# A selective scan on one core: three of sixteen products u·B per chunk move to GpSimd, its products with C are written in place in a ring of eight states, and C is broadcast and copied two states later

## The reference, cut to what matters

```python
dt = softplus(dt_low @ dt_proj_w.T + dt_proj_b)
dA = exp(dt[..., None] * A)
dBx = dt[..., None] * Bc[:, :, None, :] * xc[..., None]
def step(h, inp):
    dA_t, dBx_t, C_t = inp
    h = dA_t * h + dBx_t
    return (h, einsum('bds,bs->bd', h, C_t))
y = ys + D * xc
y = y * silu(z)
```

## Time and profile before

| | |
|---|---|
| median of 3 executions | 6006.07 us (6005.42 to 6010.8) |
| the profiled execution, its own time | 5990.85 us |
| its span | 5989.1 us |
| DVE busy in the span | 5104.7 us (85%) |
| PE busy | 4802.9 us (80%) |
| ACT busy | 3730.3 us (62%) |
| POOL busy | 1754.4 us (29%) |
| the scan of the first image | from 228 to 702 us |

### The profile page before, as it was taken

One profiled execution on the slowest core, in us unless ns is written; L12 is line 12 of the kernel. 1 busy time (PEld: TensorE's weight loads), 2 busy tenths in 40 slices (PEclk: granted clock), 3 DMA queues, 4 the chain that ended last, 5 costly groups with the idle time before them and its releaser, 6 DMA issues. The chain is left out here.

```text
span 5989.1 us, 76415 instructions
## 1 busy us (share of the span) xinstructions
PE 4802.9 (80%) x21528; PEld 1760.4 (29%) x21592; DVE 5104.7 (85%) x6562; ACT 3730.3 (62%) x4769; POOL 1754.4 (29%) x1306
## 2 busy tenths in 40 slices
PE   5767779998666777999867677799986767789997
PEld 2222422223322242222332224222233222422223
DVE  6799779998779977999868996799987899679998
ACT  1666368883266636888326663788832666378882
POOL 3488500000148850000014885000001588400000
PEclk8899989999889998999988999899988899989998
DMA  1000020000000002000000000200000000020000
GB/s 38 0 1 0 15 54 0 0 0 22 22 0 1 0 15 54 0 0 0 22 22 0 1 0 15 54 0 0 0 22 22 0 1 0 15 54 0 0 0 15
DMA packets 26646, 69.25 MB, mean 12 GB/s; under 512 B 11224, under 2 KB 13088, under 8 KB 23328
## 3 DMA queue, kind: packets, MB, share of 16 engines
q1 hardware_dynamic: 26400, 66.43, 4.4%
HBM read 26.55 MB, written 8.39 MB: 6 GB/s over the span
## 5 line engine op out<-in xcount | busy, mean ns | idle before, releaser
L1257 ACT ACTIVATE arena<-ps 128x1024 f32<-128x1024 f32 x2048 | 1982.8, 1024 | 282.7 <-PE ps L1228 242.0
L1272 DVE TENSOR_TENSOR arena<-arena 128x1024 f32<-128x1024 f32 x1664 | 1913.9, 1220 | 130.3 <-ACT arena L1257 130.2
L916 DVE TENSOR_TENSOR_SCAN arena<-ps,hlast,arena 128x512 f32<-128x512 f32 x1024 | 1267.3, 1281 | 5.2 <-DVE arena L898 3.2
L876 POOL TENSOR_TENSOR arena<-arena 128x1024 f32<-128x1024 f32 x512 | 1206.9, 2357 | 22.6
L1228 PE MATMUL ps<-arena 128*128 (+1 forms) x4096 | 1079.8, 384 | 87.5 <-issue 61.6
L1212 PE MATMUL ps<-arena 128*32 128x512 f32 x8192 | 1077.0, 603 | 38.2 <-DVE arena L1277 35.2
L845 ACT ACTIVATE ps<-arena,amat 128x512 f32<-128x512 f32 x1024 | 692.0, 688 | 508.2 <-DVE arena L916 507.5
L813 PE MATMUL ps<-arena,ident 128*128 128x512 f32 x2048 | 970.2, 597 | 7.7 <-POOL arena L876 7.7
L1572 POOL MEMSET arena<- 128x1024 f32 x4 | 3.8, 956 | 2771.8 <-POOLq L101 2771.8
L1228 PEld LDWEIGHTS ps<-arena 128*128 128x128 f16 x4096 | 316.1, 98 | 1194.6 <-ACT arena L1257 807.1
L898 DVE TENSOR_TENSOR arena<-arena,ps 128x1024 f32<-128x1024 f32 x512 | 618.4, 1208 | 45.2 <-remote 30.9
(11 more groups left out here) (242 smaller groups left out, 4402.5 us busy)
## 6 DMA issues: line engine op xcount, KB each, us to landing
arena<-x SPq DMA_DIRECT2D x32, 512.0 KB, 5.9
arena<-arena SPq DMA_DIRECT2D x64, 256.0 KB, 6.0
arena<-arena SPq DMA_DIRECT2D x64, 224.0 KB, 5.8
arena<-pe SPq DMA_DIRECT2D x256, 32.0 KB, 1.8
out<-arena SPq DMA_DIRECT2D x8, 1024.0 KB, 3.9
expw<-L_ffn_expert_w SPq DMA_DIRECT2D x1, 512.0 KB
wqkv<-L_attn_W_qkv SPq DMA_DIRECT2D x1, 192.0 KB
wx<-in_projT SPq DMA_DIRECT2D x1, 128.0 KB
```

The lines of the kernel that those rows point to most:

```text
L876: pool.tensor_tensor(halves(g[s % 4]), halves(hb[s % 4]), cs[s % 4].unsqueeze(1).broadcast_to([128, HD, CH]), ALU.mult).then_inc(hc_s, 1)
L916: dve.tensor_tensor_scan(halves(hb[s % 4])[:, h, :], da(s, h), halves(dbx[s % 2])[:, h, :], k.hlast[:, s, h, :], ALU.mult, ALU.add).then_i ...
L1257: act.activation(probs[p % 8], k.bank(2 * group[p], 2 * CH), ACT.Exp, scale=SCALE / SPLIT ** 2).then_inc(exp_s, 1)
L1272: dve.tensor_tensor(acc[p % 2], acc[p % 2], probs[p % 8], ALU.add).then_inc(acc_s, 1)
```

## The change

POOL now also computes the products u·B of states 8, 12 and 15 ("lent" states). For each, PE broadcasts B_s into the bank of C, ACT copies it to SBUF (`bs`), and POOL multiplies it with u into one of two new tiles (`dbp`), from which DVE scans. `LOANED` gives for each of these states the step in which B is spread and copied, and the step after whose product with C POOL does the multiplication. The states stand in a ring of eight tiles, and POOL writes h·C over the state itself. ACT, not POOL, saves the last column. C_s is broadcast and copied at step s+2, and `total` comes six states later instead of four. The pieces of the next chunk's preparation stand at other states: rounding behind state 4 (was 8), the three softplus parts behind 6, 8 and 10 (were 10, 11, 12), 1+x at 3 (was 7), Ln at 6 (was 10).

```diff
-    dbx, hb, g = low[0:2], low[2:6], low[6:10]
+    dbx, hb = low[0:2], low[2:10]
+    RING, LATE, CLATE = len(hb), 6, 2
...
+    LOANED = {8: (2, 2), 12: (5, 7), 15: (8, 9)}
+    SOFTPLUS = (6, 8, 10)
...
 # tensor
+                    if s - 1 in spread_at:
+                        pe.wait_ge(lent_s, lent(c, spread_at[s - 1]) + 1)
...
+                    if s >= CLATE:
+                        spread_c(c, s - CLATE, q)
...
+                    if s >= LATE:
+                        total(c, s - LATE)
...
+                    if s in spread_at:
+                        pe.matmul(k.bank(C_BANK), k.sel[:, spread_at[s], :], pieces[q], start=True, stop=True).then_inc(lent_mm, 1)
             chunks(body, pe)
-            for s in range(DS - 4, DS):
+            for s in range(DS - CLATE, DS):
+                spread_c(NCH - 1, s, 1)
+            for s in range(DS - LATE, DS):
                 total(NCH - 1, s)
...
 # scalar
+                    act.activation(k.hlast[:, (s - 2) % DS, :, :], halves(hb[(s - 2) % RING])[:, :, CH - 1:CH], ACT.Copy).then_inc(hl_s, 1)
+                    if s >= CLATE:
+                        copy_c(c, s - CLATE)
...
+                    if s in spread_at:
+                        p = spread_at[s]
+                        act.wait_ge(lent_mm, lent(c, p) + 1)
+                        act.wait_ge(lent_dbx, lent(c, p) + (2, 0, 1)[loans.index(p)])
+                        act.activation(bs[loans.index(p) % 2], k.bank(C_BANK), ACT.Copy).then_inc(lent_s, 1)
...
 # gpsimd
-                    pool.tensor_copy(k.hlast[:, s, :, :], halves(hb[s % 4])[:, :, CH - 1:CH]).then_inc(hl_s, 1)
...
-                    pool.tensor_tensor(halves(g[s % 4]), halves(hb[s % 4]), cs[s % 4].unsqueeze(1).broadcast_to([128, HD, CH]),
+                    pool.tensor_tensor(halves(hb[s % RING]), halves(hb[s % RING]), cs[s % 4].unsqueeze(1).broadcast_to([128, HD, CH]),
                                        ALU.mult).then_inc(hc_s, 1)
+                    if s in inject_at:
+                        p = inject_at[s]
+                        wait(lent_s, lent(c, p) + 1)
+                        pool.tensor_tensor(halves(dbp[loans.index(p) % 2]), halves(u[q]), bs[loans.index(p) % 2].unsqueeze(1).broadcast_to([128, HD, CH]),
+                                           ALU.mult).then_inc(lent_dbx, 1)
...
 # vector
-                        if h == 0 and s < DS - 1:
+                        if h == 0 and s < DS - 1 and s + 1 not in LOANED:
                             inject(c, q, s + 1)
-                    if more and s == 8:
+                    if more and s == 4:
                         steps.vector_rounding(dve, c + 1)
-                    if s == 2 and not first(c):
+                    if s == LATE - 2 and not first(c):
                         finish(c - 1)
```

More of the change, by code:

```diff
@@ L549, in __init__ @@
         self.ab, self.onep, self.rx = take(HD * CH), take(HD * CH), take(HD * CH)
-        self.rest = self.onep[:, 0:CH]
+        self.rest = take(CH)
         self.pieces = [take(CH // 2).bitcast(BF16) for _ in range(2)]
@@ L776, in scan, with owned, lent @@
     low = [k.at(a, HD * CH) for a in range(DBC_AT + L, STEPS_AT, HD * CH)]
-    dbx, hb, g = low[0:2], low[2:6], low[6:10]
+    dbx, hb = low[0:2], low[2:10]
+    RING, LATE, CLATE = len(hb), 6, 2
     cs = [low[10 + i // 2][:, (i % 2) * CH:(i % 2 + 1) * CH] for i in range(4)]
-    assert steps.end <= ARENA
+    bs = [low[12][:, i * CH:(i + 1) * CH] for i in range(2)]
+    dbp = [k.at(steps.end + i * HD * CH, HD * CH) for i in range(2)]
+    assert steps.end + 2 * HD * CH <= ARENA
+    LOANED = {8: (2, 2), 12: (5, 7), 15: (8, 9)}
+    SOFTPLUS = (6, 8, 10)
+    loans = sorted(LOANED)
+    spread_at = {LOANED[p][0]: p for p in loans}
+    inject_at = {LOANED[p][1]: p for p in loans}
+    NL, OWN = len(loans), DS - len(loans)
+    def owned(s):
+        return s - sum(p < s for p in loans)
+    def lent(c, p):
+        return c * NL + loans.index(p)
     dt, u, pieces, dt_s, rx_s, pc_s = steps.dt, steps.u, steps.pieces, steps.dt_s, steps.rx_s, steps.pc_s
@@ L783, in scan @@
         "b_mm", "c_mm", "y_mm", "da_ready", "dbx_ready", "scan_done", "hlast_saved", "hc_ready", "c_copied", "chunk_done"))
+    lent_mm, lent_s, lent_dbx = (k.sem(n) for n in ("lent_b_mm", "lent_b_copied", "lent_dbx_ready"))
     def da(s, h):
@@ L806, in total @@
             def total(c, s):
-                pe.wait_ge(hc_s, c * DS + (s + 5))
+                pe.wait_ge(hc_s, c * DS + (s + 1))
                 if s == 0:
@@ L812, in total, with spread_c @@
                 for h in range(HD):
-                    last = pe.matmul(k.bank(Y_BANK + h), k.ident[:, :], halves(g[s % 4])[:, h, :], start=False, stop=s == DS - 1)
+                    last = pe.matmul(k.bank(Y_BANK + h), k.ident[:, :], halves(hb[s % RING])[:, h, :], start=False, stop=s == DS - 1)
                 last.then_inc(y_mm, 1)
+            def spread_c(c, s, q):
+                if s >= 1 or not first(c):
+                    pe.wait_ge(cs_s, c * DS + s)
+                pe.matmul(k.bank(C_BANK), k.sel[:, DS + s, :], pieces[q], start=True, stop=True).then_inc(c_mm, 1)
             def body(c, q, more):
@@ L838, in _, with copy_c @@
         def _(act):
+            def copy_c(c, s):
+                n = c * DS + s
+                act.wait_ge(c_mm, n + 1)
+                if s >= 4 or not first(c):
+                    act.wait_ge(hc_s, n - 3)
+                act.activation(cs[s % 4], k.bank(C_BANK), ACT.Copy).then_inc(cs_s, 1)
             def body(c, q, more):
@@ L845, in body @@
                         act.activation(da(s, h), halves(dt[q])[:, h, :], ACT.Exp, scale=k.amat[:, h, s:s + 1]).then_inc(da_s, 1)
[L846 to L852, removed]
+                    act.activation(k.hlast[:, (s - 2) % DS, :, :], halves(hb[(s - 2) % RING])[:, :, CH - 1:CH], ACT.Copy).then_inc(hl_s, 1)
+                    if s >= CLATE:
+                        copy_c(c, s - CLATE)
+                    elif not first(c):
+                        copy_c(c - 1, s - CLATE + DS)
+                    if s in spread_at:
[3 more added lines that the diff above has]
+                        act.activation(bs[loans.index(p) % 2], k.bank(C_BANK), ACT.Copy).then_inc(lent_s, 1)
                     if more and s < HD:
@@ L855, in body @@
                     if more and s == 2:
+                        steps.scalar_high(act, c + 1, 1 - q)
                         steps.scalar_exp(act, c + 1)
                     if more and s == 3:
+                        steps.scalar_one_plus(act, c + 1)
+                    if more and s == 5:
                         steps.scalar_middle(act, c + 1, 1 - q)
-                    if more and s == 7:
-                        steps.scalar_one_plus(act, c + 1)
-                    if more and s == 10:
+                    if more and s == 6:
                         steps.scalar_log(act, c + 1)
+            act.wait_ge(k.sem("h_zero"), 3)
             chunks(body, act)
+            for s in range(DS - CLATE, DS):
+                copy_c(NCH - 1, s)
         @block.gpsimd
@@ L881, in body @@
                         steps.pool_low(pool, c + 1, 1 - q)
[L882 to L888, removed]
+                    if more and s in SOFTPLUS:
+                        steps.pool_softplus(pool, c + 1, 1 - q, SOFTPLUS.index(s))
+            for last in hb[RING - 2:RING]:
+                pool.memset(halves(last)[:, :, CH - 1:CH], 0.0).then_inc(k.sem("h_zero"), 1)
+            pool.memset(k.hlast[:, 0:DS - 2, :, :], 0.0).then_inc(k.sem("h_zero"), 1)
+            pool.wait_ge(k.sem("h_zero"), 3)
+            pool.sem_inc(hl_s, DS - 2)
             chunks(body, pool)
```

45 lines of the change are left out of this document (25 added, 20 removed).

## The result

| | before | after |
|---|---|---|
| median | 6008.43 us (6005.42 to 6010.87) | 6113.15 us (6109.96 to 6118.54) |
| span of the profiled execution | 5989.1 us | 6108.1 us |

The ratio is 1.0175, with a 95% interval of 1.0158 to 1.0193. The change makes the kernel slower by about 105 us. The forecast was 64 us faster, and its range ended at 5977.

A forecast was written before the change was run, and what follows sets the result against it. DVE was taken to set the pace in the scan. Injects -107, rounding +39, image ends +14 and image starts -10 sum to -64 us, so 6006 became 5942, rounded to 5943, with a range of 5900 to 5977.

The forecast's parts named there:

- What bounds the kernel, and the injects: Scan: DVE sets the pace; three injects less save 3.33 us a chunk, 107 us in all, period 54.9.
- POOL's rate: Scan: POOL operations follow every 2.30 us, in place too; 52.8 us a chunk fits under 54.9, load 96%.
- the lower bound of 0.1: Column copy on ACT: taken as 0.2 us, bounded by 0.1 and 0.3.
- The moved rounding: Behind state 4, DVE's rounding sits out one POOL operation: 1.4 us a chunk, 39 us given back over 28 roundings.
- the bound of 2.2: Most the rounding would lose a chunk, in us, if a POOL operation starts just ahead of it.
- The end of an image: Six sums queued behind the last C broadcast: finish starts 8.5 us after the scans, 14 us lost in all.
- The start: First chunk of each image: DVE's 14.3 us wait goes as C comes later; gain 10 us, bounds 0 and 14.
- No collision: Rival, 15%: a POOL boundary falls by the rounding, so all 39 us stay: 5904.
- "slower" rival: Rival, 5%: ten POOL operations from product 6 to next chunk's u hold back the inject of state 0: 6020.

The follow-up runs named there:

- the first two experiments: Changed kernel with one rounding input in PSUM, its correction left out: 5912.06 us; changed kernel with POOL waiting for the rounding before lent product 8: 5918.62 us.
- the experiment with the old places: Changed kernel with the rounding, Ln and three softplus parts back at the states where they stood before: 6151.94 us, ratio 1.0254.
- the last one: Changed kernel with POOL waiting before lent product 8, finish ahead of the rounding, and two sums earlier at an image's end: 5903.83 us, ratio 0.9845.

## Why the prediction was wrong, point by point

- **What bounds the kernel, and the injects: right.** DVE sets the pace in the scan, and with the stretch taken away the chunk runs as forecast: where POOL waits ahead of the lent product of state 8, the roundings of two chunks without a wait for B start at 412.76 and 467.55 (54.8 apart; 54.9 was forecast).
- **POOL's rate: right.** Its operations keep the spacing of 2.30, in place too, and its mean load fits: busy for 53.18 of those 54.79 us, 97% where 96% was given. The column copy on ACT, for which 0.2 was taken, has a mean of 191 ns, but the copy of C starts 0.1 behind its start (300.51 and 300.60 in the changed kernel), so it adds the lower bound of 0.1. The first product of the chunk starts 11.0 into it, where 10.9 was given.
- **The moved rounding: the step that failed.** "The rounding must sit out the rest of it and ends near 20.0 instead of 18.6: 1.4 a chunk." The place and the partner of the collision were right (ready at 17.43 in the chunk against 17.4, in the lent product of state 8), and also the cause, shown by the kernel with one operand in PSUM. The length was not. The text itself names POOL's operations there "all back to back", and yet prices one of them. The price came from the project stage, where an idle time of 0.27 and 0.18 stands before POOL's operations, as each waits for the one ahead. In the scan there is no gap between POOL's operations, as the earlier trace rows shows (338.80 comes 2.31 behind 336.49, which lasts 2.35). In all 28 chunks of the changed kernel DVE got in only when POOL ran dry, and the bound of 2.2 that I gave as the highest was none. Measured: a stretch of 6.5 a chunk, 181 us in all where 39 stood in the sum. The kernel with a gap between two POOL operations brings the stretch to 1.8 a chunk (89.7 us for its 32 executions), near the forecast's 1.4.
- **Who waits for the delayed instruction: not followed.** `finish` is queued behind the rounding, the first sum waits for it on PE, and the sum runs at the lower clock, so that B comes late. That was 46.5 us of waits, absent from the prediction's sum. The kernel with `finish` first shows where they come from: with the rounding between `finish` and the inject, 7 are left. Why the clock is low there is not shown. Not all of it is owed to the stretch: with a rounding of 1.2 us in the same place 20.0 were left.
- **The end of an image: right.** 34.0 us of idle time ahead of the four last `finish`, 8.5 each, as forecast. **The start: right** as far as the old wait goes: the 14.3 us of the earlier trace rows are gone from the first chunk, all of them, where the sum took 10.
- **The rivals.** "No collision" is what the first two experiments made, at 5912 and 5919, by the ratio 5923 and 5930 (5904 was given, without the waits for B). The "slower" rival named another mechanism, POOL's chain to u. It did not act in the changed kernel, but does in the experiment with the old places (78.7 us) and, by 1.4 us, in the last one. The rival that should have stood there is the collision itself, with the number of POOL operations in the run as its size.

With the measured stretch and the waits in it, the sum of the prediction is -107 + 181 + 32 + 14 = +120, against +119 in the spans.

## What to carry to other kernels

Before GpSimd is filled, look for each VectorE instruction with both inputs in SBUF: beside a GpSimd run without gaps it can last as long as the run, so price it by the number of operations that will follow each other, not by one. Letting GpSimd wait for that instruction where it has idle time ahead cost little here and removed it. One operand in PSUM removed it too, but that was run only with the rounding's correction left out. A duration read in another stage carries that stage's gaps with it; check that the neighbours' idle times are the same before using it.

## What the runs showed of the hardware

- A DVE operation of 1.2 us with two SBUF inputs took 1.20 to 1.25 us beside an idle POOL, 1.63 to 3.39 beside one POOL operation, 2.23 to 3.39 with more behind it after a gap, and 6.24 to 8.00 beside runs of three without a gap. It ended 1.1 behind the last POOL operation that it had to wait for. With one input in PSUM it took 1.19 to 1.22 beside a POOL at work. The Trainium skill ("SBUF — State Buffer", section "Who interferes with whom") says that the first to issue gets the shared pair for the whole instruction. Every collision here agrees with that, but the 7.36 us show that POOL can keep it from one instruction to the next when they follow without a gap; by the rule alone, with DVE next in turn, an estimate is 2.8 (309.54, the end of the lent product, plus 1.08, less 307.86). POOL did not always keep it: in 4 collisions of the experiment with the old places DVE came in between two operations without a gap in the records (2.17 to 2.20).
- The granted clock of TensorE was 0.50, the 1.2 GHz level, from 316 to 320, behind 9.03 us without work, and the sum's first two matmuls (four records) took 3.75 us there. At the other level they took 1.95 to 1.98, in the kernel before behind 1.79 to 1.90 us without work. The last idle time alone does not tell which it will be: 3.52 behind 1.80 us in the changed kernel, and 3.64 behind 2.13 but 1.98 behind 2.65 in two chunks of one run.
